# Windowed convolution with four wide tiles and one small one cut into four column phases, and the up-sampled band ahead of the next image set

## The chip, the core and the metric

The kernel runs on one core of one Trainium2 chip. The metric is the device time of one execution in microseconds, median over runs. PE is TensorE, DVE VectorE, ACT ScalarE, POOL GpSimd, SP the engine that here only issues DMAs.

## What is computed

The input x is (8, 96, 256, 256) in float32. Two layers are added to it in turn: y = x + L0(groupnorm(x)), a windowed linear attention with a batch norm, and out = y + L1(groupnorm(y)). The change touches L1 alone:

```python
for i in range(3):                      # three Haar levels
    co = haar2d(cur)                    # ll, lh, hl, hh at half the size
    cur = co[:, :, 0]
    flat = dwconv(co.reshape(B, 4 * C, h, w), wconv_w[i]) * wscale[i]      # 5x5, per channel
    level_coeffs.append(flat.reshape(B, C, 4, h, w))
next_ll = zeros
for i in reversed(range(3)):
    next_ll = ihaar2d(level_coeffs[i].at[:, :, 0].add(next_ll))
out = y + dwconv(gn_y, base_w) * base_scale + base_b + next_ll
```

## The kernel before

It has three stages. The first few tens of us build coefficient vectors (`pads`, written to `vec1` to `vec3` in DRAM by L270 to L272) and take statistics of the first image. The second, to about 5530 us, is layer 0; it writes y to `y_scratch`. The third, from about 5570 us to the end, is layer 1, and the change lies in it, but for the layout of `vec1`.

The third stage goes channel by channel, each channel in two sets of four images: 192 groups. `loop_groups` runs the same body (`steps`) on PE, ACT and DVE, each engine in its written order, joined by semaphores. An even group is the first set of a channel, an odd group the second. Level 1 and the base convolution are merged: on the full-size image they act as a 5x5 operation over pairs of rows and columns. The 256 rows are cut in five windows (`WINDOWS`), each with 52 output rows in a tile of 64 rows with halo. The two column phases (even, odd columns) lie in partitions 0 to 63 and 64 to 127, so that one tile is 128 partitions by 4 images x 128 columns = 512 elements. Each convolution of a tile (`conv(t)`) is 5 column taps x 3 matmuls (`split`, L1292 to L1294: high x high, high x low, low x high parts of a float32) = 15 matmuls of 512 columns.

One group on each engine, in order:

- PE: conv(0), conv(1); level 3 (L1325 to L1334, 20 matmuls); level 2 (30 matmuls of 256 columns); conv(2) to conv(4); a wait for `next_lo` (L1340); the up-sampling of the low band into the five windows (L1344, L1346, six matmuls of 512 columns); a wait for all five `z_lo` (L1297) and `sum_down` of the next group (L1300, ten matmuls of 512 columns into `ps_ll`).
- ACT: copy of `ps_ll` (L1263), the high parts of the level inputs (L1265, L1267), `norm` of the next group (L1243: 16 instructions from `x1` into `z`), `leading` of the next group (L1256, L1258: high parts), copy of level 3 (L1273), the high parts of the up-sampled band (L1277, L1278).
- DVE: `finish` of window 0 of the group before (L1438, two instructions a window, into `ob`), `make_in` (L1392, L1395), `finish` of window 1, `split_in` (L1402), `finish` of windows 2 to 4, `make_x1` for two groups ahead (L1369: x + gain * y), `trailing` of the next group (L1382, L1385: low parts), `up_levels` (L1409 to L1419), `split_next` (L1424, L1426; it sets `next_lo`).
- POOL, once a channel: `build` of the first level's weights when their raw DMAs have landed, and of the weights of levels 2 and 3 when level 2 of the odd group has been computed (`l2_ready`): L1185 and L1193.
- SP, in one queue: for each group, wait for `make_x1` two ahead, ten loads (`load`, L1130) for three ahead, the gain, then the five stores of this group (`store`, L1141), each behind its `finish`, which runs in the next group's turn. After an odd group's stores: the parameters, a wait for the weights of levels 2 and 3, and ten raw DMAs (`load_raw`, L1111, L1116, L1120). So the raw DMAs are issued in the turn of an even group, and that group's loads stand behind them in the queue; they are the data of the `make_x1` in the following odd group.

`xb`, `yb`, `ob` and `z` are single buffers; `zb` is double by set; `x1` has four slots.

Of the kernel before, what the change touches and what calls it, by code (L numbers as in the profile page):

```python
# [21 lines left out]
F32 = mybir.dt.float32  # L22
F32R = mybir.dt.float32r
ALU = mybir.AluOpType
# [19 lines left out]
TAPS = 5  # L44
HALF = W // 2
WROWS = 64
# [9 lines left out]
NV1 = 4 * TAPS * 2  # L56
# [7 lines left out]
CHUNKS = PIECE // 512  # L64

# [8 lines left out]
def wt_attention_kernel(nc, x, wqkv_t, wp_t, gamma, beta, base_w, base_b, base_scale, wconv, wscale,  # L74
# [10 lines left out]
    with ExitStack() as ctx:  # L85
# [128 lines left out]
        with ExitStack() as ph:  # L214
# [62 lines left out]
            def _(pool):  # L277
# [30 lines left out]
                p1 = pad1.rearrange("p (ia q dj o n) -> p ia q dj o n", ia=2, q=2, dj=TAPS, o=2)  # L308
                for ia in range(2):
                    for q in range(2):  # L310
                        for oa in range(2):
                            for p in range(2):
                                o = 1 - p
                                first = WROWS - 3 - oa
                                full = p1[:, ia, q, :, o, first:first + 2 * TAPS - 1:2]
# [5 lines left out]
                                for n, dj in enumerate(djs):  # L321
                                    lo = first + 2 * dis[0]
                                    part = p1[:, ia, q, dj, o, lo:lo + 2 * len(dis) - 1:2]
# [672 lines left out]
        with ExitStack() as ph:  # L996
# [14 lines left out]
            x1 = [sb_(f"x1_{s}", [128, PAIRW, IMGS, W]) for s in range(SLOTS)]  # L1011
# [3 lines left out]
            zb = [[sbr_(f"zb{g}_{h}", [128, WINDOWS, IMGS, ZW]) for h in range(2)] for g in range(SETS)]  # L1015
            raw1 = sb_("raw1", [128, 2 * TAPS, WROWS])
            raw2 = sb_("raw2", [128, 2 * TAPS, HALF])
            raw3 = sb_("raw3", [128, 2 * TAPS, HALF])
            mat1 = [[sbr_(f"mat1_{k}_{h}", [128, TAPS, 2 * WROWS]) for h in range(2)] for k in range(2)]
            mat2 = [sbr_(f"mat2_{h}", [128, 2, TAPS, HALF]) for h in range(2)]  # L1020
# [3 lines left out]
            down_sb = sbr_("down_sb", [128, WINDOWS, HALF])  # L1024
            UPPER = -(-(HALF // 2) // (OROWS // 2))
            LOWER = WINDOWS - HALF // OROWS
            up_sb = sbr_("up_sb", [128, UPPER + LOWER, 2 * WROWS])
            inside_sb = sb_("inside_sb", [128, PAIRW])
            mask = sb_("mask", [128, 2])
            zero1 = sb_("zero1", [128, 1])  # L1030
            z = sb_("z", [128, WINDOWS, IMGS, HALF])
# [21 lines left out]
            const_in, zeroed = sem_("constc_in"), sem_("zeroed")  # L1053
            xy_in, down_set, mask_set = sem_("xy_in"), sem_("down_set"), sem_("mask_set")
# [14 lines left out]
            NRAW = (4 + 2 + 4) * 16  # L1069
            GROUPS_C = C * SETS  # L1070

            def zero_pads(eng):
# [10 lines left out]
            def slot(k, g):  # L1083
                return 2 * k + g
# [452 lines left out]
```

## Time and profile before

| | us |
|---|---|
| median of 3 runs (lowest, highest) | 11057.21 (11053.29, 11059.47) |
| the profiled execution, its own time | 11061.64 |
| its span | 11059.8 |
| PE busy in the span | 10538.7 |
| DVE busy | 9242.7 |
| ACT busy | 7168.6 |
| POOL busy | 3679.7 |

The busy times are of the whole span, and the stages differ, so the third stage is read by itself, in a timeline of two groups. An instruction's duration counts its latency: matmuls overlap, and the pitch from one start to the next is what one costs. Times in the timelines are from the start of the span.

### The profile page before, as it was taken

Reading aid. Unit: us, or ns where it says so; the run is one execution under the profiler, and the core shown is the slowest. Engines: PE = TensorE matmul, PEld = TensorE weight load, DVE = VectorE, ACT = ScalarE, POOL = GpSimd, SP = SyncE. Lnnn points to the kernel's source line nnn. Section 1 sums busy time; section 2 is a strip of 40 time slices with the busy share of each in tenths; the row PEclk is TensorE's granted clock in tenths of the full one; section 3 lists DMA queues with packets and bytes.
Section 4 is the critical chain, followed back from the end, with each engine's and each line's share of the span. In section 5 each row is a group of like instructions: output and inputs, shape, how many; then the busy total and the mean of one; then the engine's idle time right before and its main releaser. Section 6 shows DMA issues by size and latency. Waiting matters only on the chain. (4 is left out here: it accounts for less than half of the span.)

```text
span 11059.8 us, 205333 instructions
## 1 busy us (share of the span) xinstructions
PE 10538.7 (95%) x66084; PEld 8946.0 (81%) x66084; DVE 9242.7 (84%) x16479; ACT 7168.6 (65%) x11852; POOL 3679.7 (33%) x3715
## 2 busy tenths in 40 slices
PE   4999999999999999999969999999999999999999
PEld 4888888888888888888858888888888888888887
DVE  6989989899998999988867777777777777777777
ACT  4777777777777777778735555555555555555554
POOL 3444444444444444444322222222222222222222
PEclk9999999999999999999979999999999999999999
DMA  5323333232333333322257777677777767767775
GB/s 185 133 92 126 109 109 126 92 130 95 126 114 104 114 103 115 126 81 74 69 124 154 155 156 154 154 152 155 156 157 157 155 153 156 155 153 154 152 156 125
DMA packets 1162861, 1453.43 MB, mean 131 GB/s; under 512 B 215391, under 2 KB 1125023, under 8 KB 1125279
## 3 DMA queue, kind: packets, MB, share of 16 engines
q1 hardware_dynamic: 1161055, 1442.80, 51.6%
q10 hardware_dynamic: 1376, 6.13, 0.1%
q8 instruction: 119, 1.95, 0.1%
q14 instruction: 311, 2.55, 0.1%
HBM read 1040.11 MB, written 408.56 MB: 131 GB/s over the span
## 5 line engine op out<-in xcount | busy, mean ns | idle before, releaser
L1292 PE MATMUL ps_w<-zb,mat 128*128 128x512 f32 x4800 | 1925.6, 401 | 8.6
L1293 PE MATMUL ps_w<-zb,mat 128*128 128x512 f32 x4800 | 1906.4, 397 | 0.0
L1294 PE MATMUL ps_w<-zb,mat 128*128 128x512 f32 x4800 | 1904.9, 397 | 0.0
L634 POOL CAST xn_hi<-xs 96x512 fp32r<-96x512 f32 x1024 | 840.7, 821 | 3112.3 <-PE ps_qkv L659 2261.1
L1438 DVE SCALAR_TENSOR_TENSOR ob<-ps_w,prm,x 64x512 f32<-64x512 f32 x1920 | 1440.5, 750 | 515.6 <-PE ps_w L1344 476.8
L1243 ACT ACTIVATE z<-x,prm 64x384 f32<-64x384 f32 (+1 forms) x3072 | 1814.0, 662 | 58.8 <-DVE x L1369 51.1
L1185 POOL CAST mat<-raw 128x1280 fp32r<-128x1280 f32 (+1 forms) x288 | 464.7, 1631 | 3947.6 <-DMA raw<-vec 2351.3
L657 PE MATMUL ps_qkv<-wqkv_hi,xn_hi 96*128 96x288 f32 x4096 | 1388.9, 339 | 38.2 <-POOL xn_lo L636 19.9
L636 POOL TENSOR_TENSOR xn_lo<-xs,xn_hi 96x512 fp32r<-96x512 f32 x1024 | 1363.4, 1331 | 81.8
L658 PE MATMUL ps_qkv<-wqkv_lo,xn_hi 96*128 96x288 f32 x4096 | 1214.1, 296 | 0.0
L659 PE MATMUL ps_qkv<-wqkv_hi,xn_lo 96*128 96x288 f32 x4096 | 1211.8, 296 | 0.0
L584 ACT ACTIVATE tok<-ps_qkv 128x1152 f32<-128x1152 f32 x1024 | 1160.6, 1133 | 0.0
L1292 PEld LDWEIGHTS ps_w<-zb,mat 128*128 128x128 f32 x4800 | 903.0, 188 | 302.9 <-DVE ob L1438 91.0
L552 ACT ACTIVATE att<-ps_t 96x512 f32<-96x512 f32 x1024 | 608.1, 594 | 805.2 <-PE ps_t L702 805.2
L687 PE MATMUL ps_g<-tok 128*104 128x97 f32 x8192 | 947.2, 259 | 160.2 <-DVE tok L795 160.1
L1294 PEld LDWEIGHTS ps_w<-zb,mat 128*128 128x128 f32 x4800 | 901.7, 188 | 227.0
L1293 PEld LDWEIGHTS ps_w<-zb,mat 128*128 128x128 f32 x4800 | 901.6, 188 | 209.3
L679 PE MATMUL ps_num<-kv_sb,q_sb 104*128 104x104 f32 x8192 | 1062.8, 273 | 0.0
L695 PE MATMUL ps_f<-att,wp_sb 96*96 96x512 f32 x2048 | 1052.6, 594 | 6.9 <-DVE f_cur_b L176 3.1
L679 PEld LDWEIGHTS ps_num<-kv_sb,q_sb 104*128 104x128 f32 x8192 | 1018.1, 192 | 0.0
L687 PEld LDWEIGHTS ps_g<-tok 128*104 128x104 f32 x8192 | 833.6, 172 | 222.4 <-DVE tok L795 219.7
L1263 ACT ACTIVATE ll<-ps_ll 128x512 f32<-128x512 f32 x192 | 114.8, 598 | 1373.4 <-PE ps_ll L1300 1373.4
(196 smaller groups left out, 24154.1 us busy)
## 6 DMA issues: line engine op xcount, KB each, us to landing
xst<-in_x SPq DMA_DIRECT2D x96, 2048.0 KB, 13.8
xs<-in_x SPq DMA_DIRECT2D x128, 1536.0 KB, 8.9
y_scratch<-ys SPq DMA_DIRECT2D x128, 1536.0 KB, 9.5
out<-ob SPq DMA_DIRECT2D x768, 208.0 KB
xb<-in_x SPq DMA_DIRECT2D x576, 256.0 KB
yb<-y_scratch SPq DMA_DIRECT2D x576, 256.0 KB
raw<-vec SPq DMA_DIRECT2D x192, 320.0 KB, 4.2
raw<-vec SPq DMA_DIRECT2D x384, 160.0 KB, 3.9
```

The costliest lines, as they stand in the source:

```text
L584: s_.activation(tok[:, slot].rearrange("p g (t c) -> p g t c", t=3)[:, :, :, 0:C], ps_qkv[:, :, 0:3 * C].rearrange("p g (t c) -> p g t c", ...
L636: nc.gpsimd.tensor_tensor(lo, pixels(xs, k, j), hi.bitcast(F32), ALU.subtract).then_inc(xlo_ready, 1)
L657: mm(o, hi, wqkv_hi[:], start=True, stop=False)
L658: mm(o, hi, wqkv_lo[:], start=False, stop=False)
L659: last = mm(o, lo, wqkv_hi[:], start=False, stop=True)
L679: last = mm(ps_num[:, g, 0:QR], q_sb[:, slot, g * 128:(g + 1) * 128], kv_sb[:, g // 2, :], start=True, stop=True)
L687: last = mm(ps_g[0:QR, w * GW:(w + 1) * GW], tok[:, slot, g, PART:PART + QR], tok[:, slot, g, 2 * PART:2 * PART + GW], start=g % 2 == 0, s ...
L1243: last = nc.scalar.activation(z[q * WROWS:(q + 1) * WROWS, ts, b, :], x1[slot(k, g)][rows, pairs, b, q::2], ACT.Identity, scale=prm[k][row ...
L1292: mm(out_, w[HI], xx[HI], start=start, stop=False)
L1293: mm(out_, w[HI], xx[LO], start=False, stop=False)
L1294: return mm(out_, w[LO], xx[HI], start=False, stop=stop)
L1438: last = v.scalar_tensor_tensor(out=ob[p:p + WROWS, t // 2].rearrange("p b w -> p (b w)")[:, q::2], in0=ps_w[t][q * WROWS:(q + 1) * WROWS, ...
```

## The change

The windows become four tiles of 64 rows and a fifth (`SPECIAL`) of 32 rows with 24 output rows. The fifth is cut in four column phases of 32 rows each, so it is 128 partitions by 4 images x 64 columns = 256 elements, and its convolution has three column taps (9 matmuls of 256 columns instead of 15 of 512). Its weights `mat_s` come from eight more raw DMAs a channel (`raw_s`, 16 partitions x 12 x 32 elements, runs of 128 B) and are built on POOL with the first level's; `vec1` gets two more column positions for it. Its normalised rows are written once as rows (`zn`, 4 ACT instructions of 32x256) and copied into the four phases (`zq`, 4 ACT copies of 32x256). Its share of the low band is not taken from the phases: POOL adds neighbouring columns of `zn` (`sum_columns`, 32x512), splits the sum into high and low, and PE sums these 32 rows with two matmuls of 512 columns. `finish` of the fifth is four instructions of 32x256.

Order: DVE finishes windows 0 and 1 ahead of `make_in`, and does `up_levels` and `split_next` ahead of `trailing`. ACT copies level 3 in the middle of `norm`, and splits the up-sampled band ahead of `leading`. `sum_down` waits tile by tile. No tile hangs over the image's edge any more, so the masks go, every `leading` is a plain copy and every `trailing` a subtraction. The constants for down- and up-sampling are computed on DVE and no longer loaded; only the pads of the buffers are cleared, and SP no longer waits for that before its first DMA of the stage.

```diff
-NV1 = 4 * TAPS * 2
+NV1 = 4 * (TAPS + 2) * 2
+SROWS = WROWS // 2
+SPHASES = 128 // SROWS
+STAPS = 3
+BLOCKS = W // SPHASES
+SPECIAL = WINDOWS - 1
+TILES = ((0, 0, WROWS - HALO), (WROWS + SROWS - 4 * HALO, HALO, WROWS - 2 * HALO),
+         (H - 2 * WROWS + 2 * HALO, HALO, WROWS - 2 * HALO), (H - WROWS, HALO, WROWS - HALO),
+         (WROWS - 2 * HALO, HALO, SROWS - 2 * HALO))
...
-                for t_ in (xb, yb, *zb[0], *zb[1], *in2_p, in3_hl):
-                    eng.memset(t_[:].bitcast(F32), 0.0).then_inc(zeroed, 1)
-                eng.memset(zero1[:], 0.0).then_inc(zeroed, 1)
+                for t_, n, width in padded_tiles:
+                    for at in (slice(0, n), slice(width - n, width)):
+                        eng.memset(t_[:].bitcast(F32)[..., at], 0.0).then_inc(zeroed, 1)
...
+                    for ia in range(2):
+                        for q in range(SPHASES):
+                            first = q * SROWS + ia
+                            sp.dma_start(raw_s[first:first + SROWS - 1:2, :, :],
+                                         bass.AP(tensor=vec1.tensor,
+                                                 offset=c * (NV1 * V1) + (((2 * ia + q % 2) * (2 * TAPS + 4) + q // 2 * 2) * V1
+                                                                          + (2 + WROWS - SROWS)),
+                                                 ap=[[2, SROWS // 2], [V1, SPHASES * STAPS], [1, SROWS]])).then_inc(raw_in, 16)
...
-                sp.wait_ge(zeroed, N_ZERO)
                 load_raw(0)
...
+                def sum_columns(qn, done, count, first=False):
+                    pool.wait_ge(done, count)
+                    pool.wait_ge(zn_set, qn + 1)
+                    if not first:
+                        pool.wait_ge(ll_ready, qn)
...
+                    nc.gpsimd.tensor_tensor(ls, rows_and_sums[SROWS:2 * SROWS, 0::2], rows_and_sums[SROWS:2 * SROWS, 1::2], ALU.add).then_inc(ls_set, 1)
...
+                    nc.gpsimd.tensor_copy(ls_hl[HI][:], ls).then_inc(ls_hi, 1)
...
+                    nc.gpsimd.tensor_tensor(ls_hl[LO][:], ls, ls_hl[HI][:].bitcast(F32),
+                                            ALU.subtract).then_inc(ls_lo, 1)
...
+                def channel(c, k):
+                    sum_columns(c * 2 + 1, mat23_ready, c + 1)
+                    build_first(c + 1, 1 - k)
+                    sum_columns(c * 2 + 2, mat1_ready, c + 2)
+                    build_levels(c + 1)
...
+                    for b in range(IMGS):
+                        img = IMGS * g + b
+                        last = nc.scalar.activation(
+                            zn[:, b], x1_s[own(k, g), b], ACT.Identity,
...
+                    last.then_inc(zn_set, 1)
                     for p in range(2):
-                        ts = slice(p, WINDOWS, 2)
-                        pairs = slice(0, len(range(p, WINDOWS, 2)))
+                        if p == 1 and between is not None:
+                            between()
+                        ts = slice(p, SPECIAL, 2)
+                        pairs = slice(0, SPECIAL // 2)
...
+                    for q in range(SPHASES):
+                        last = nc.scalar.activation(zq[q * SROWS:(q + 1) * SROWS].rearrange("p b j -> p (b j)"),
+                                                    rows_and_sums[SROWS:2 * SROWS, q::SPHASES], ACT.Copy)
...
-                    if n is None or n + 1 < GROUPS_C:
-                        m1, k1, g1 = ahead(m, k, g, 1)
-                        norm(m1, k1, g1)
-                        leading(qn + 1, g1)
-                    act.wait_ge(l3_ready, qn + 1)
...
+                    if more:
+                        norm(m1, k1, g1, between=copy_s3)
+                    else:
+                        copy_s3()
                     act.wait_ge(next_ready, qn + 1)
...
+                    if more:
+                        leading(qn + 1, g1)
...
                 def sum_down(qn, g):
-                    pe.wait_ge(z_lo, qn * WINDOWS + WINDOWS)
-                    for t in range(WINDOWS):
+                    for t in range(SPECIAL):
+                        pe.wait_ge(z_lo, qn * WINDOWS + (t + 1))
...
+                    pe.wait_ge(ls_lo, qn + 1)
+                    for h in (HI, LO):
+                        last = mm(ps_ll[:], down_sb[0:SROWS, SPECIAL, :], ls_hl[h][:], start=False, stop=h == LO)
                     last.then_inc(ll_ready, 1)
...
+                        if t == SPECIAL:
+                            for d in range(STAPS):
+                                split(ps_w[t][:, 0:IMGS * BLOCKS], [mat_s[k][h][:, d, :] for h in range(2)],
+                                      [zs[g][h][:, :, d:d + BLOCKS] for h in range(2)], d == 0, False)
+                            return
...
-                        finish(qn - 1, mb, kb, gb_, (0,))
+                        finish(qn - 1, mb, kb, gb_, (0, 1))
                     make_in(qn)
                     if before:
-                        finish(qn - 1, mb, kb, gb_, (1,))
+                        finish(qn - 1, mb, kb, gb_, (2,))
                     split_in(qn)
                     if before:
-                        finish(qn - 1, mb, kb, gb_, range(2, WINDOWS))
+                        finish(qn - 1, mb, kb, gb_, (3, 4))
                     if n is None or n + 2 < GROUPS_C:
                         make_x1(*ahead(m, k, g, 2))
+                    up_levels(qn)
+                    split_next(qn)
                     if n is None or n + 1 < GROUPS_C:
                         trailing(qn + 1, ahead(m, k, g, 1)[2])
-                    up_levels(qn)
-                    split_next(qn)
```

## Rows read from the trace of the kernel before

**Rows 1.** The page, part 1: busy time, share and instructions of each engine.

```profile
PE 10538.7 (95%) x66084; PEld 8946.0 (81%) x66084; DVE 9242.7 (84%) x16479; ACT 7168.6 (65%) x11852; POOL 3679.7 (33%) x3715
```

**Rows 2.** Busy time by stretches: engines' busy us (instructions), PEclk, DMA share, GB/s.

```profile
8000.00:11000.00 3000.00, 2963.87 (x14997) 2449.22 (x14996) 2344.48 (x3408) 1670.30 (x2868) 795.47 (x857) 1.00 0.71 154
```

**Rows 3.** Timeline of PE over an even group: start, us, then the instruction.

```profile
8006.38 0.97 PE L1344 MATMUL ps_w<-next_a,up_sb 128*128 128x512 f32 x3 [1.30 <-DVE next_b L1426]
...
8010.27 0.39 PE L1292 MATMUL ps_w<-zb,mat 128*128 128x512 f32 x1
...
8017.65 0.28 PE L1332 MATMUL ps<-in_hl,mat 128*128 128x256 f32 x1
...
8020.02 0.28 PE L1292 MATMUL ps<-in,mat 128*128 128x256 f32 x1
...
8023.66 0.40 PE L1292 MATMUL ps_w<-zb,mat 128*128 128x512 f32 x1
...
8034.23 0.86 PE L1344 MATMUL ps_w<-next_a,up_sb 128*128 128x512 f32 x3
...
8035.63 2.53 PE L1300 MATMUL ps_ll<-zb,down_sb 128*128 128x512 f32 x10
8038.00 0.39 PE L1292 MATMUL ps_w<-zb,mat 128*128 128x512 f32 x1
```

**Rows 4.** Timeline of DVE, the same group and the odd one behind it.

```profile
8015.03 4.61 DVE L1438 SCALAR_TENSOR_TENSOR ob<-ps_w,prm,x 64x512 f32<-64x512 f32 x6
8019.56 3.66 DVE L1369 SCALAR_TENSOR_TENSOR x<-yb,gain,xb 128x1024 f32<-128x1024 f32 x3
...
8023.81 1.88 DVE L1385 TENSOR_TENSOR zb<-z,zb 128x512 fp32r<-128x512 f32 x3
...
8026.28 0.41 DVE L1409 TENSOR_TENSOR sum<-s 128x256 f32<-128x256 f32 x1
...
8027.33 0.42 DVE L1415 TENSOR_TENSOR low<-up,ps 128x256 f32<-128x256 f32 x1
...
8055.01 1.47 DVE L1409 TENSOR_TENSOR sum<-s 128x256 f32<-128x256 f32 x1
...
8058.12 0.42 DVE L1415 TENSOR_TENSOR low<-up,ps 128x256 f32<-128x256 f32 x1
...
8060.02 1.20 DVE L1424 TENSOR_TENSOR next_a<-next_ll,next_a 64x512 fp32r<-64x512 f32 x1 [0.70 <-ACT next_a L1277]
```

**Rows 5.** Groups of ACT's instructions by form, 6000 to 9000 us: busy us, mean ns.

```profile
L1243 ACT ACTIVATE z<-x,prm 64x256 f32<-64x256 f32 x848 | 452.4, 605 | 2.8
...
L1267 ACT ACTIVATE in_hl<-in 128x256 fp32r<-128x256 f32 x107 | 44.1, 412 | 0.0
```

**Rows 6.** Timeline of POOL, the odd group: weights of levels 2 and 3.

```profile
8051.73 4.48 POOL L1185 CAST mat<-raw 128x1280 fp32r<-128x1280 f32 x2 [17.42 <-PE ps L1294]
8056.39 7.95 POOL L1193 TENSOR_TENSOR mat<-raw,mat 128x256 fp32r<-128x256 f32 x10 [0.18 <-POOL mat L1185]
```

**Rows 7.** Timeline of SP's queue in the even group: start and us of the issue.

```profile
8008.69 11.52 SPq L1141 DMA_DIRECT2D out<-ob  x5
...
8020.89 3.20 SPq L1111 DMA_DIRECT2D raw<-vec  x4
...
8029.24 0.36 SPq L1130 DMA_DIRECT2D xb<-in_x  x1
...
8030.26 0.66 SPq L1130 DMA_DIRECT2D xb<-in_x  x1
```

**Rows 8.** Busy time by stretches, as rows 2, where that group's loads end.

```profile
8042.00:8044.00 2.00, 2.00 (x10) 1.56 (x10) 1.95 (x4) 1.99 (x4) 0.00 (x0) 1.00 0.91 201
8044.00:8046.00 2.00, 2.00 (x13) 1.73 (x12) 1.92 (x4) 1.99 (x4) 0.00 (x0) 1.00 0.52 168
```

**Rows 9.** Timelines at the start of the third stage: POOL's clearing, SP's first raw DMA.

```profile
5569.57 2.66 POOL L1075 MEMSET xb<- 128x3072 f32 x1 [69.52 <-POOLq L885]
...
5586.53 2.73 SPq L1111 DMA_DIRECT2D raw<-vec  x4
```

More of the change, by code:

```diff
@@ new lines, in build_first @@
+                def build_first(c, k, first=False):
+                    pool.wait_ge(raw_in, c * NRAW + NRAW)
+                    if not first:
+                        pool.wait_ge(out_ready, c * (2 * WINDOWS) + (LEAD - 2 * WINDOWS))
+                    pool.sem_inc(pool_turn, 1)
+                    build([(mat1[k], raw1[:].rearrange("p (d o) m -> p d (o m)", o=2)[:, :, ::-1], "p d m -> p d m"),
+                           (mat_s[k], raw_s[:].rearrange("p (d o) m -> p d (o m)", o=SPHASES)[:, :, ::-1],
+                            "p d m -> p d m")],
+                          mat1_hi, mat1_ready, c + 1)
@@ L1211, in loop_groups @@
+                sum_columns(0, zeroed, N_ZERO, True)
+                build_first(0, 0, True)
+                build_levels(0)
+                with pool.Fori(0, C // 2 - 1) as m:
+                    for k in range(2):
+                        channel(m * 2 + k, k)
+                channel(C - 2, 0)
+                sum_columns(C * 2 - 1, mat23_ready, C)
             def loop_groups(eng, steps):
@@ L1436, in finish @@
                                 dve.wait_ge(prm_in[k], mc * 16 + 16)
-                        for q in range(2):
+                        for q in range(SPHASES if t == SPECIAL else 0):
+                            last = v.scalar_tensor_tensor(
+                                out=ob[0:SROWS, t // 2].rearrange("p b w -> p (b w)")[:, q::SPHASES],
+                                in0=ps_w[t][q * SROWS:(q + 1) * SROWS, 0:IMGS * BLOCKS], scalar=prm[k][own(k, g), 1:2],
+                                in1=x1_s[own(k, g)].rearrange("p b w -> p (b w)")[:, q::SPHASES],
+                                op0=ALU.add, op1=ALU.add)
+                        for q in range(0 if t == SPECIAL else 2):
                             last = v.scalar_tensor_tensor(
@@ L1471, in _ @@
[L1471 to L1476 removed]
+                v.memset(down_sb[:].bitcast(F32), 0.0).then_inc(down_set, 1)
+                v.memset(up_sb[:].bitcast(F32), 0.0).then_inc(down_set, 1)
@@ new lines, in _ @@
+                for rows, at in ((0, UPPER_AT), (64, LOWER_AT)):
+                    for t in at:
+                        start, skip, n = TILES[t]
+                        width = tile_place(t)[2]
+                        src = ident_sb[rows:rows + 64, (start + skip) // 2:(start + skip + n) // 2]
+                        for q in range(128 // width):
+                            which = at[t] + (q // 2 if t == SPECIAL else 0)
+                            for to in (0, 64):
+                                o = up_sb[to:to + 64, which, q * width + skip:q * width + skip + n]
+                                v.tensor_scalar(o.rearrange("p (a r) -> p a r", r=2), src.unsqueeze(2).to_broadcast(
+                                    [64, n // 2, 2]), 0.5, None, ALU.mult).then_inc(down_set, 1)
```

186 lines of the change are left out of this document (100 added, 86 removed).

## The prediction, written before the changed kernel was run

> **What bounds the kernel now.** I read the page first, for the engines' shares [rows 1], then the third stage alone, where the change lies: in 3000 us of it PE is busy for 2964 us, DVE for 2344, at the full clock, and the DMA engines are busy for 0.71 [rows 2]. The stretch holds 14997 matmuls and a group has 141 (75 of the convolution, 20 of level 3, 30 of level 2, 6 up, 10 down), so a group takes 28.2 us and a pair of groups (one channel) 56.4 us. Then the timeline of PE over one even group: from its first convolution at 8010.27 to the next group's at 8038.00 are 27.7 us without a wait to speak of [rows 3]. The odd groups make up the rest; ahead of 8006.38 PE stood 1.3 us for the up-sampled band, `next_lo` [rows 3]. The reason is on POOL, which builds the weights of levels 2 and 3 in the odd group, 4.5 + 7.95 us from 8051.73 on [rows 6]: in that time DVE's way from `sum` to `low2` takes 3.1 us instead of 1.05, and a subtraction of 512 elements 1.20 instead of about 0.65 [rows 4]. So PE sets the time, and the other engines' chains are late by a little, in odd groups alone.
>
> **PE.** The pitch of a 512-column matmul is (8034.23 - 8023.66) / 45 = 0.235 us, that of a 256-column one (8023.66 - 8020.02) / 30 = 0.121 us [rows 3]. The fifth window's 15 matmuls of 512 columns become 9 of 256: 3.52 - 1.09 = 2.43 us less. Up-sampling goes from 6 x 0.235 to 5 x 0.235 + 2 x 0.121, no change. `sum_down` keeps ten matmuls of 512 columns; I cost 32 instead of 128 rows at nothing. Conv(0) and conv(1) took 8017.65 - 8010.27 = 7.38 us for 30 x 0.235 = 7.05; the 0.33 is conv(1)'s wait for window 1's `finish`, which now comes ahead of `make_in` and fills DVE's wait for the down-sum. PE's work in a group is then 27.73 - 2.43 - 0.33 = 24.97 us, a pair 49.9. That is the floor, 6.5 us under 56.4. The question is who now comes late. I count from T, the end of `sum_down`. PE reaches level 3 at T + 7.05, ends it at 9.4 and level 2 at 13.05, wants `next_lo` at 21.2 and the first `z_lo` at 22.6.
>
> **ACT, even group.** Copies and level inputs end at T + 2.6. `zn` is four Identity instructions at 0.605 us or less [rows 5], overlapping by some 0.07: 2.15 us. The first half of `norm` is eight of them, 4.3 us, to T + 9.0; level 3's copy waits for PE's T + 9.4, to 10.1; the second half ends at 14.4, four `zq` copies of at most 0.41 [rows 5] at 15.9. Only then come the two splits of the band, to T + 17.2, and `leading`, one tile every 0.55. ACT's sum is some 18 us of 25, so the new instructions are hidden; were they twice as dear, the splits would end near T + 20, still ahead of PE.
>
> **DVE, even group.** The `finish` of windows 2 to 4 ended at 8015.03 + 4.61, T + 9.4 [rows 4]. One window of 1.5 us moves into the earlier wait; the fifth costs four instructions of 256 elements, bounded by half and all of 0.77 each, 1.5 to 3.1 us. I take 1.7 because the 256-element addition from PSUM is 0.42 [rows 4]. `finish` ends near T + 8.0, `make_x1` (3.66) near 11.7, `up_levels` waits for level 2 at 13.05 and gives the band at 14.4. ACT's splits then set `next_lo` at T + 18. `trailing` is 0.65 a tile (1.88 for three, overlapped [rows 4]), so `z_lo` of tile 3 comes at 20.6. PE wants them at 21.2 and 24: no stall. Even group: 25.0 us.
>
> **POOL.** `sum_columns` is two additions or subtractions of 512 elements and a cast. Its bounds are one and two times a 256-element operation (0.80 [rows 6]) each, and 0.9 for the cast (2.24 for 1280): 2.5 to 4.1 us a group, from T + 4.7 to 8.8 at the latest. PE wants it at T + 24. It contends with `split_in` for about a us, and level 3 has 2 us of room. The weights of the first level and of the fifth tile are ready long before the next channel.
>
> **SP, and the odd group.** This is what I expect to come late. The even group's stores end at 8008.69 + 11.52 = T + 9.9; the raw DMAs start at T + 10.6, the loads at 8029.24, 8.35 us later [rows 7]. Now `finish` and the last store come 1.3 us earlier, but eight raw DMAs more stand in front of the loads. No row has their form; an issue costs 0.36 to 0.80 us [rows 7]. They move 192 runs each, nearer to the load of 60 rows (240 runs, 0.36) than to `raw1` (320 runs, 0.80), with a gap: I take 0.5, so 4.0 us (2.9 to 6.4). The loads start at T + 9.3 + 8.35 + 4.0 = 21.65. Before, they had landed when the DMA share fell from 0.91 to 0.52, near 8044.7 [rows 8], 15.5 us after the first issue, two stores of this turn among them (about 2 us); with 288 rows for 304 and the stores behind them I take 13 us (12.2 to 15). That is T + 34.65, or 9.7 us after the odd group's own T', where `make_x1` could start at 8.0: DVE waits 1.7 us (0 to 6). `make_x1` ends at T' + 13.4. Now POOL is building (its start is level 2's end plus 0.4, T' + 13.4, for 12.6 us). From `sum` to the splits are 8060.02 - 8055.01 = 5.0 us, and 2.4 for the two: `next_lo` at T' + 20.8, just in time. But `trailing` now stands behind it, within POOL's build, at 1.2 us a tile: 22.0, 23.2, 24.4, 25.6 for PE's wishes 22.6 to 24.0. `sum_down` ends 0.94 after the last: T' + 26.6. Odd group 26.6, a stall of 1.6. A pair takes 51.6 us, 4.8 less; times 96: 461 us.
>
> Before, in the same place, `trailing` lay ahead of the band and was hidden under the convolution; the new order trades a late `next_lo` for a late `z_lo`.
>
> The Trainium skill, "SBUF — State Buffer", section "Who interferes with whom", says that a DVE instruction with two SBUF inputs and a GpSimd one exclude each other for the whole instruction. The slowed `sum` beside the unslowed `low2`, which reads PSUM, agrees [rows 4]; the price taken is the row's.
>
> **Start of the stage.** SP's first raw DMA waited for POOL's clearing, 5569.57 to 5586.53 [rows 9]. That wait goes, 17 us; the eight raw DMAs cost 4 back, and DVE's small constants lie under the loads. The chain from the loads to the first matmul is otherwise the same: 12 us saved (0 to 17). The longer `vec1` at the very start lies beside the statistics' loads: 0 to 3 us, taken as 0.
>
> **Sum.** 11061.6 (the profiled execution) - 461 - 12 = 10588. It stands 4.4 us above the median; so 10585.
>
> **The rivals.** (a) The raw DMAs are cheap or the loads land sooner, DVE doesn't wait, and even `trailing` is in time: the floor, 96 x 6.5 = 624 us off, 10425. For it: the DMA engines are busy for only 0.71 [rows 2]. Against: even with no wait of `make_x1`, `trailing` runs in POOL's build. (b) The queue is slower: 0.80 an issue and 15 us to land. The wait is 6 us, `next_lo` comes at T' + 25 and the odd group takes 29.3: a pair 54.3, 202 us off, 10845; with half of that, 10720. (c) DVE and POOL alternate whole instructions in `trailing`: 0.65 + 0.80 a tile instead of 1.2 is 1.0 us more a pair, 10680. (d) Slower than before: the same wait, past the point where it eats all. A us of it costs 96 us once `next_lo` is late; the pair is at 56.4 when the wait is 8.3 us, the loads landing at T' + 16.3. It takes 1.3 us an issue, or 128-byte runs that hold the DMA engines as long as 1 KB ones. At a wait of 10 us the pair is 58.1: 11210. Against: no issue in the rows costs 1.3.
>
> The Trainium skill, "DMA: Bandwidth & Descriptors", section "Specifications", gives 512 B as the least transfer at line rate, with a read-modify-write below. It speaks for (b) and (d); `raw_s` has the shortest runs of the kernel, and no row of before has 128 B.
>
> **How the numbers follow.** Forecast 0.45 (its own range 10500 to 10690), (a) 0.2, (b) 0.2, (c) 0.09, (d) 0.06. The range reaches from the floor to the middle of (b) and somewhat beyond: 10430 to 10800. 0.2%, some 22 us, is about what a measurement can tell from no change; the cases give faster 0.93, same 0.01, slower 0.06.
>
> **What would show it.** Right: even groups of 25.0 us without a wait; in odd ones DVE waits 1 to 3 us for the DMAs ahead of L1369's successor, `next_lo` isn't waited for, and PE waits in front of `sum_down` for `zb`'s low parts, 1 to 2 us. The raw issues on SP sum to about 12 us. Wrong: PE waits in even groups too, or for POOL's column sum, the issue of `raw_s` above 0.8, or a pitch of the small convolution's matmuls above 0.121.

## The result and the profile after

The changed kernel takes 11172.8 us (median of four runs, 11163.8 to 11186.5), the kernel before 11055.3 us on the same chip. The ratio is 1.011, its 95% interval 1.0095 to 1.0125. The change makes the kernel 1.1% slower, where 10585 us, some 4% faster, was forecast. The profiled execution took 11171.4 us, with a span of 11169.6.

The page of the kernel after, part 1 (busy time, share and instructions of each engine), and the first line of part 4 (the chain of work that ended last, by engine):

```profile
PE 10330.1 (92%) x65124; PEld 8796.7 (79%) x65124; DVE 9545.6 (85%) x16891; ACT 7837.5 (70%) x13388; POOL 4581.3 (41%) x4591
...
SPq 16%; DVE 15%; DMA 7%; PE 6%; issue 6%; ACT 1%; DVEq 0%; ACTq 0%
```

PE has 209 us less to do than in [rows 1], in spite of a longer run. So the work was saved, and it no longer sets the time. Before, the same line of part 4 was:

```profile
PE 28%; DVE 16%; issue 4%; ACT 1%; DMA 0%; SPq 0%; POOL 0%; DVEq 0%; POOLq 0%
```

Each chain covers about half of the span. PE had 28% of the span on it and SP's queue nothing; now SP's queue and DVE have 31%, and PE 6%.

Busy time of each engine in the same stretch of 3000 us, with the columns of [rows 2]:

```profile
8000.00:11000.00 3000.00, 2782.83 (x14095) 2313.29 (x14094) 2448.92 (x3529) 1989.37 (x3629) 1264.68 (x1298) 0.94 0.70 150
```

PE is busy for 2783 us instead of 2964, and the granted clock, 1.00 before, is 0.94. The waits between 6000 and 9000 us (engine, line and releaser: us in total, times, longest) say where it stands:

```profile
ACT ll L1336 <- PE ps_ll L1383: 534.1, 104, 6.3
...
PE ps_w L1434 <- DVE next_b L1513: 216.6, 52, 5.0
DVE x L1459 <- DMA yb<-y_scratch: 200.1, 52, 4.9
```

The first line has one wait a group: 104 groups in 3000 us, so a pair of groups takes 57.7 us (56.4 before, 51.6 forecast). The two below come 52 times, once a pair: DVE waits 3.85 us for the loads of `make_x1` (L1459), and PE 4.17 us for the band, `next_lo` (L1434). The timeline of PE shows a pair, an even group first and the odd one behind it (start, us of the instruction, idle time ahead of it):

```profile
7987.80 0.50 PE L1371 MATMUL ps_w<-zb,mat 128*128 128x512 f32 x1
...
8009.13 0.62 PE L1434 MATMUL ps_w<-next_a,up_sb 128*128 128x512 f32 x2
...
8010.73 2.08 PE L1379 MATMUL ps_ll<-zb,down_sb 128*128 128x512 f32 x8
8012.74 0.72 PE L1383 MATMUL ps_ll<-ls,down_sb 32*128 32x512 f32 x2
8013.39 0.50 PE L1371 MATMUL ps_w<-zb,mat 128*128 128x512 f32 x1
...
8034.60 0.28 PE L1373 MATMUL ps_w<-zs,mat_s 128*128 128x256 f32 x1
8039.84 1.22 PE L1434 MATMUL ps_w<-next_a,up_sb 128*128 128x512 f32 x2 [4.96 <-DVE next_b L1513]
...
8042.61 3.08 PE L1379 MATMUL ps_ll<-zb,down_sb 128*128 128x512 f32 x8
...
8046.28 0.50 PE L1371 MATMUL ps_w<-zb,mat 128*128 128x512 f32 x1
```

The even group takes 8013.39 - 7987.80 = 25.6 us and has no such wait. The odd one takes 8046.28 - 8013.39 = 32.9 us: 4.96 of waiting, and then 6.44 us for the up- and down-sampling that took 8013.39 - 8009.13 = 4.26 us in the even group. The stretches of two us around it say why (columns as above; the last three numbers are granted clock, DMA share, GB/s):

```profile
8036.00:8038.00 2.00, 0.00 (x0) 0.00 (x0) 1.28 (x3) 1.17 (x2) 2.00 (x4) 1.00 1.11 212
8038.00:8040.00 2.00, 0.16 (x1) 0.16 (x1) 1.96 (x3) 1.98 (x5) 2.00 (x3) 0.53 1.15 204
8040.00:8042.00 2.00, 2.00 (x5) 1.61 (x6) 2.00 (x3) 0.61 (x2) 0.38 (x1) 0.50 1.13 208
...
8044.00:8046.00 2.00, 2.00 (x8) 1.30 (x6) 1.95 (x3) 0.00 (x0) 0.00 (x0) 0.77 1.13 207
8046.00:8048.00 2.00, 2.00 (x9) 1.42 (x8) 0.99 (x4) 0.78 (x2) 0.00 (x0) 1.00 0.82 216
```

PE has stood still since 8034.88; from 8038 on it is granted 0.50, the 1.2 GHz level, and it has the full clock back in the stretch that begins at 8046. The wait is paid once as a wait and once more, 2.2 us, as slow matmuls.

What made the band late is read from SP's queue, then DVE, then POOL. SP, as in [rows 7], from the channel's first raw DMA to the first load, and the same place a pair later:

```profile
7997.97 3.01 SPq L1137 DMA_DIRECT2D raw<-vec  x4
8001.16 5.97 SPq L1144 DMA_DIRECT2D raw_s<-vec  x8
8007.33 1.48 SPq L1150 DMA_DIRECT2D raw<-vec  x2
8008.99 2.79 SPq L1154 DMA_DIRECT2D raw<-vec  x4
8012.11 0.62 SPq L1164 DMA_DIRECT2D xb<-in_x  x1
...
8056.34 3.01 SPq L1137 DMA_DIRECT2D raw<-vec  x4
```

DVE, the odd group, then `make_x1` of the next even group, where POOL is idle:

```profile
8027.15 4.28 DVE L1459 SCALAR_TENSOR_TENSOR x<-yb,gain,xb 128x1024 f32<-128x1024 f32 x2 [4.42 <-DMA yb<-y_scratch]
8031.46 1.64 DVE L1459 SCALAR_TENSOR_TENSOR x_s<-yb,gain,xb 32x1024 f32<-32x1024 f32 x1
8033.13 0.84 DVE L1496 TENSOR_TENSOR sum<-s 128x256 f32<-128x256 f32 x1
...
8038.66 1.13 DVE L1513 TENSOR_TENSOR next_b<-next_ll,next_b 64x512 fp32r<-64x512 f32 x1
8039.82 2.92 DVE L1472 TENSOR_TENSOR zb<-z,zb 128x512 fp32r<-128x512 f32 x4
...
8052.38 2.74 DVE L1525 SCALAR_TENSOR_TENSOR ob<-ps_w,prm,x_s 32x256 f32<-32x256 f32 x4
8055.15 2.48 DVE L1459 SCALAR_TENSOR_TENSOR x<-yb,gain,xb 128x1024 f32<-128x1024 f32 x2
8057.66 1.28 DVE L1459 SCALAR_TENSOR_TENSOR x_s<-yb,gain,xb 32x1024 f32<-32x1024 f32 x1
```

POOL, the weights of levels 2 and 3, as in [rows 6]:

```profile
8026.90 3.45 POOL L1219 CAST mat<-raw 128x1280 fp32r<-128x1280 f32 x2 [1.45 <-PE ps L1373]
8030.54 9.84 POOL L1227 TENSOR_TENSOR mat<-raw,mat 128x256 fp32r<-128x256 f32 x10 [0.18 <-POOL mat L1219]
```

A line of several instructions (`x8`) runs from the first start to the last end, gaps included. The eight new DMAs take 5.97 us of SP's queue so, and 6.2 to the start of the next DMA. The loads then start 24.3 us after the even group's T = 7987.80 and let DVE go at 8027.15, 15.0 us later. That is the moment when POOL begins its build, and `make_x1`, beside the casts and the first subtractions, takes 5.95 us instead of the 3.79 of 8055.15 to 8058.94. The band's second split ends at 8039.79, 26.4 us after T' = 8013.39, and PE was through with its convolution at 21.5.

**It closes to a circle.** From raw DMA to raw DMA: 14.1 us to the first load, 15.0 to `make_x1`, 6.0 for it, 6.7 to the end of the splits, 15.3 for `trailing`, the next group's inputs and `finish` up to 8055.12, and 1.2 for the last store and the parameters to 8056.34. From 7997.97 to 8056.34 that is 58.4 us, this pair's length (8046.28 - 7987.80 = 58.5 on PE), and PE's saved matmuls aren't on it. The steps between the splits and the end of `finish` lean on PE only through the down-sampled copy, for which DVE waits about 1 us. One more step of the circle has grown with the change: `finish` of the fifth tile, four instructions in 2.74 us, where a window in two took 1.5 ([rows 4]: 4.61 for three). No run takes that away by itself.

### The profile page after: what moved, and what is told of

The parts are those of the page before. It is cut to its first block, busy times and chain, and to the rows that moved or that the text cites. A ratio compares the mean times of both kernels' runs of the same rounds, so it can differ in the third digit from the quotient of the medians.

```text
span 11169.6 us, 210512 instructions
## 1 busy us (share of the span) xinstructions
PE 10330.1 (92%) x65124; PEld 8796.7 (79%) x65124; DVE 9545.6 (85%) x16891; ACT 7837.5 (70%) x13388; POOL 4581.3 (41%) x4591
## 4 chain that ended last, share of the span: by engine, by line
SPq 16%; DVE 15%; DMA 7%; PE 6%; issue 6%; ACT 1%; DVEq 0%; ACTq 0%
DMA yb<-y_scratch 7%; SPq L1164 5%; SPq L1144 4%; DVE x L1459 3%; PE ps_ll L1379 2%; SPq L1137 2%; DVE ob L1525 2%; SPq L1154 2%; DVE ob L1531 2%; DVE x_s L1459 2%; SPq L1150 1%; PE ps_w L1436 1%; PE ps_w L1434 1%; DVE next_b L1513 1%; DVE sum L1496 1%
## 5 line engine op out<-in xcount | busy, mean ns | idle before, releaser
L1317 ACT ACTIVATE z<-x,prm 64x256 f32<-64x256 f32 x3072 | 1640.6, 605 | 15.1
L1371 PE MATMUL ps_w<-zb,mat 128*128 128x512 f32 x3840 | 1546.6, 403 | 1.2 <-DVE ob L1531 1.2
L1373 PE MATMUL ps_w<-zb,mat 128*128 128x512 f32 x3840 | 1526.6, 398 | 0.0
L1372 PE MATMUL ps_w<-zb,mat 128*128 128x512 f32 x3840 | 1524.8, 397 | 0.0
L1531 DVE SCALAR_TENSOR_TENSOR ob<-ps_w,prm,x 64x512 f32<-64x512 f32 x1536 | 1151.5, 750 | 34.9 <-PE ps_w L1434 5.1
L1227 POOL TENSOR_TENSOR mat<-raw,mat 128x256 fp32r<-128x256 f32 (+1 forms) x1248 | 1155.6, 959 | 34.7 <-POOL mat_s L1219 17.4
L801 DVE TENSOR_REDUCE ss<-sq 128x64 f32<-128x768 f32 x1024 | 965.8, 943 | 18.2 <-ACT sq L594 17.7
L717 PEld LDWEIGHTS ps_t<-ident_sb,att_t 128*96 128x96 f32 x4096 | 480.7, 125 | 612.4 <-issue 611.7
L1459 DVE SCALAR_TENSOR_TENSOR x<-yb,gain,xb 128x1024 f32<-128x1024 f32 x384 | 585.4, 1565 | 407.6 <-DMA yb<-y_scratch 404.6
## 6 DMA issues: line engine op xcount, KB each, us to landing
xst<-in_x SPq DMA_DIRECT2D x96, 2048.0 KB, 13.8
```

The source lines that it names most:

```text
L1317: last = nc.scalar.activation(z[q * WROWS:(q + 1) * WROWS, ts, b, :], x1[slot(k, g)][rows, pairs, b, q::2], ACT.Identity, scale=prm[k][row ...
L1371: mm(out_, w[HI], xx[HI], start=start, stop=False)
L1372: mm(out_, w[HI], xx[LO], start=False, stop=False)
L1373: return mm(out_, w[LO], xx[HI], start=False, stop=stop)
L1531: last = v.scalar_tensor_tensor(out=ob[p:p + WROWS, t // 2].rearrange("p b w -> p (b w)")[:, q::2], in0=ps_w[t][q * WROWS:(q + 1) * WROWS, ...
```

## The experiments

Two theories stood at first. By the **queue theory** the eight DMAs ahead of the loads make `make_x1` late, and this sets the time. By the **port theory** DVE and POOL hold each other up, and the order in which the loads come matters little. Ratios are to the kernel before on the same chip, with their 95% intervals. The edits are to the kernel after unless said otherwise.

**The raw DMAs moved behind the loads.** In SP's program, inside the even group, and taken out at the end of the channel:

```diff
                         if g == 0 and more:
                             load_gain(m * 2 + (k + 2), k)
+                    if g == 0 and raw:
+                        sp.wait_ge(mat23_ready, m * 2 + (k + 1))
+                        load_raw(m * 2 + (k + 1))
                     store(m * 2 + k, g, m * 4 + (2 * k + g))
...
                         load_prm(m * 2 + (k + 2), k)
-                        sp.wait_ge(mat23_ready, m * 2 + (k + 2))
-                        load_raw(m * 2 + (k + 2))
```

> The changed kernel, with the eighteen raw DMAs of an even group issued behind that group's ten loads instead of ahead of them. Queue theory (the odd group is late because its data stand behind the raw DMAs): the loads start some 8 us earlier, DVE's wait for them in front of make_x1 (200 us in 3000 us) goes, the odd group falls from 32.9 to 25 to 28 us, the whole to 10,450 to 10,800 us. Port theory (the odd group is late because DVE and POOL want SBUF together while POOL builds): the wait for the loads goes, but the odd group keeps 30 us or more and the whole stays above 10,950. The weights come later here, so a wait of level 3 for them would be a cost of this edit of its own.

It took 11027.4 us, ratio 0.9992 (0.9982 to 1.0001): 1.2% off the kernel after, and no more. DVE no longer waits for loads, and PE no longer for the band. But the weights now arrive late, and their build slides into the odd group's `trailing`. DVE, then POOL, in that place, and one wait of PE:

```profile
8039.87 6.13 DVE L1471 TENSOR_TENSOR zb<-z,zb 128x512 fp32r<-128x512 f32 x4
...
8049.88 1.48 DVE L1478 TENSOR_TENSOR in<-ll 128x256 f32<-128x256 f32 x2
```

```profile
8040.95 3.37 POOL L1218 CAST mat<-raw 128x1280 fp32r<-128x1280 f32 x2
8044.50 8.20 POOL L1226 TENSOR_TENSOR mat<-raw,mat 128x256 fp32r<-128x256 f32 x10 [0.18 <-POOL mat L1218]
```

```profile
PE ps_ll L1378 <- DVE zb L1471: 73.1, 116, 0.9
```

Four tiles of `trailing` take 6.13 us, 1.5 each, where they took 2.92 in the kernel after; `in<-ll` takes 1.48 instead of 0.77. Moving the queue's load turned a late transfer into a longer overlap of DVE and POOL. The queue is a cause, but undoing it in this way pays back the gain; each theory was half right.

**The eight DMAs left out** (only channels 0 and 1 fetch them; the others use the fifth tile's weights of channel 1):

```diff
+                    if not small:
+                        sp.sem_inc(raw_in, 8 * 16)
-                    for ia in range(2):
+                    for ia in range(2 if small else 0):
                         for q in range(SPHASES):
```

> The changed kernel, with the eight raw_s DMAs issued for channels 0 and 1 only; later channels use the fifth tile's weights of channel 1, so the output is not the reference's. It takes away 6.0 us of issue and the 128-byte runs, and leaves the order as it is. Queue theory: the loads start 6 us earlier, DVE's wait falls from 3.9 us in an odd group to nothing, and the whole to 10,550 to 10,750 us. Port theory: the whole falls by less than 250 us.

10714.7 us, ratio 0.9711 (0.9694 to 0.9727). By the two ratios that is 0.0399 x 11055 = 441 us less than the kernel after. The waits for the loads and for the band are gone from the head of the list, and the clock in the stretch is 1.00. The eight DMAs alone, issue and transfer together, cost 441 / 96 = 4.6 us a pair.

**The wait replaced by work.** If PE's wait is only a symptom of the circle, 20 more matmuls in its place cost nothing; and if the half clock behind it matters, they even win:

```diff
+                    if g == 1:
+                        pe.wait_ge(ll_copied, qn + 1)
+                        for _i in range(20):
+                            mm(ps_ll[:], down_sb[:, 0, :], zb[g][HI][:, 0, :, 2:2 + HALF], start=True, stop=True)
                     pe.wait_ge(next_lo, qn + 1)
```

> The changed kernel, with 20 matmuls of 512 columns into the free ps_ll put in front of PE's wait for the up-sampled band in odd groups, 4.7 us of work that nobody uses. Clock theory (after the 5 us wait PE runs at half its clock for some 6 us more, which costs 2.2 us an odd group): the wait becomes work of the same length, the granted clock stays at 1.0, and the whole falls by about 96 x 2.2 = 210 us, to 10,960. If the slower matmuls had another cause, or the clock no part in it, the time stays at 11,170 or rises.

11097.2 us, ratio 1.0054 (1.0037 to 1.007). The timeline of PE at that place, and DVE's wait from 6000 to 9000 us:

```profile
8011.03 4.88 PE L1430 MATMUL ps_ll<-zb,down_sb 128*128 128x512 f32 x20
8016.18 0.73 PE L1438 MATMUL ps_w<-next_a,up_sb 128*128 128x512 f32 x2 [0.28 <-DVE next_b L1517]
...
8017.88 2.08 PE L1379 MATMUL ps_ll<-zb,down_sb 128*128 128x512 f32 x8
```

```profile
DVE x L1463 <- DMA yb<-y_scratch: 256.5, 53, 5.4
```

PE now stands still for 0.28 us, `sum_down` runs at full speed (2.08 instead of 3.08), and yet only 75 us are won (62 by the ratios), 0.8 a pair at most, not the 2.2 that the half clock costs PE. DVE simply waits longer for the loads, 4.8 us instead of 3.85. This is the plainest evidence for the circle: PE can be given 4.9 us more work in every pair, and the kernel gets faster. The little that is won fits DVE's wait for the down-summed copy, which from 6000 to 9000 us fell from 86.8 to 58.2 us. My expectation took the clock's 2.2 us for time on the path; only the 1 us for which DVE waits on PE's down-sum was.

**The eight DMAs added to the kernel before**, in the same place of SP's queue, into memory that has no use in this stage:

```diff
                     for ia in range(2):
+                        for q in range(4):
+                            first = q * 32 + ia
+                            sp.dma_start(extra[first:first + 31:2, :, :],
+                                         bass.AP(tensor=vec1.tensor,
+                                                 offset=c * (NV1 * V1) + (((2 * ia + q % 2) * 8 + q // 2 * 2) * V1 + 34),
+                                                 ap=[[2, 16], [V1, 12], [1, 32]])).then_inc(raw_in, 16)
+                    for ia in range(2):
```

> The kernel before, with eight more raw DMAs of the form of raw_s (16 partitions, 12 runs of 128 B) a channel, in the place in the queue where the changed kernel has them, into a space that nobody reads any more. Queue theory: the loads of the even group start 6 us later, the next odd group's make_x1 waits 3 to 5 us for them and slides into POOL's build, and PE waits in odd groups: the whole rises by 150 to 700 us over the kernel before, which has a longer group (28.2 us) and so some 3 us more room. If the queue is harmless, the time stays within 50 us of the kernel before.

11445.5 us, ratio 1.0356 (1.0339 to 1.0374). SP's queue, then DVE:

```profile
8021.37 5.97 SPq L1120 DMA_DIRECT2D outer<-vec  x8
...
8032.12 0.37 SPq L1139 DMA_DIRECT2D xb<-in_x  x1
```

```profile
8047.26 3.67 DVE L1378 SCALAR_TENSOR_TENSOR x<-yb,gain,xb 128x1024 f32<-128x1024 f32 x3 [1.49 <-DMA yb<-y_scratch]
```

The same 5.97 us, the same 15 us to land (8032.12 to 8047.26), and a wait of `make_x1` that the kernel before doesn't have in its odd group:

```profile
8047.29 3.66 DVE L1369 SCALAR_TENSOR_TENSOR x<-yb,gain,xb 128x1024 f32<-128x1024 f32 x3
```

The eight cost 401 us, 4.2 a pair, without any other part of the change. `make_x1` itself is not slowed in this place (3.67 us against 3.66), so this is the queue's part almost by itself.

**Most of the contention taken away.** Levels 2 and 3 built with two subtractions instead of ten from the second channel on, so that the other low parts stay those of the first channel:

```diff
-                        for d in range(0, raw.shape[1], 2):
+                        for d in range(0, 2 if light else raw.shape[1], 2):
```

> The changed kernel, with POOL's build of the weights of levels 2 and 3 cut from ten subtractions to two from the second channel on (the other low parts stay those of channel 0, so the output is not the reference's). The queue is as it is. Queue theory alone: the loads land as late as before, make_x1 starts as late, the time falls by less than 200 us. Port theory alone: without POOL beside them make_x1, the way from sum to low2 and the splits of the odd group take their undisturbed times, 5 to 6 us less, PE's wait goes and with it the half clock, and the whole falls by 500 us or more, to 10,650. I expect both: what lies beside the eight subtractions left out is some 4 us of DVE, so 10,700 to 10,850.

10947.3 us, ratio 0.9909 (0.9893 to 0.9926): 225 us, less than I had expected. The waits between 6000 and 9000 us:

```profile
DVE x L1459 <- DMA yb<-y_scratch: 218.2, 54, 5.2
...
PE ps_w L1434 <- DVE next_b L1513: 148.7, 55, 3.1
```

DVE waits for the loads as in the kernel after. The two casts, which lie right over `make_x1`, were left in (its instructions of 128x1024 average 1.58 us in both kernels), and so was the queue.

**The new order undone**: `trailing` ahead of the band again, and on ACT `norm` and `leading` ahead of level 3's copy and the splits.

```diff
-                    up_levels(qn)
-                    split_next(qn)
                     if n is None or n + 1 < GROUPS_C:
                         trailing(qn + 1, ahead(m, k, g, 1)[2])
+                    up_levels(qn)
+                    split_next(qn)
```

> The changed kernel with the old order: DVE does trailing ahead of up_levels and split_next, ACT does all of norm and leading ahead of level 3's copy and the band's splits. The tiles, the raw DMAs and the column sum stay. In the odd group make_x1 ends late either way; with trailing (3 to 5 us) in front, the band comes later by that, and PE's wait for it grows from 5 to 8 to 10 us: the whole rises by 200 to 450 us, to 11,400 to 11,600. If the new order were what costs, the time would fall towards 10,900 instead.

11740.6 us, ratio 1.0625 (1.0608 to 1.0643). The wait for the band, from 6000 to 9000 us:

```profile
PE ps_w L1432 <- DVE next_b L1511: 450.8, 95, 8.2
```

It now comes in every group, even ones too. The new order isn't the cause; without it the change costs 568 us more.

**The eight DMAs on ACT's queue**, four at the end of each group, after `leading`. The function is SP's own loop, with the engine as an argument:

```diff
                     if more:
                         leading(qn + 1, g1)
+                    if g == 0 and (n is None or 0 < n < GROUPS_C - 2):
+                        load_raw_s(act, m * 2 + (k + 1), (1,))
+                    if g == 1 and (n is None or n < GROUPS_C - 4):
+                        act.wait_ge(mat1_ready, m * 2 + (k + 2))
+                        load_raw_s(act, m * 2 + (k + 2), (0,))
```

> The changed kernel with the eight raw_s DMAs issued by ACT, four at the end of each group, so that SP's queue holds what it held before the change; every byte still moves and the output is the reference's. Queue theory, by issue: the loads start 6 us earlier, as when the eight are left out (10,715), DVE's wait for them goes; ACT, with 7 us of room in a group, pays 3: 10,700 to 10,820, a kernel faster than both by 2 to 3%. If it is the transfer of the 128-byte runs that made the loads late, and not their issue, the wait stays and the time is above 11,000.

10896.9 us, ratio 0.9858 (0.9841 to 0.9874), 1.4% under the kernel before with all its output. Timeline of DVE in the odd group, then one of the new issues on ACT:

```profile
8032.22 2.91 DVE L1468 SCALAR_TENSOR_TENSOR x<-yb,gain,xb 128x1024 f32<-128x1024 f32 x2
...
8043.68 4.55 DVE L1481 TENSOR_TENSOR zb<-z,zb 128x512 fp32r<-128x512 f32 x4
```

```profile
8015.81 0.63 ACTq L1123 DMA_DIRECT2D raw_s<-vec  x1
```

`make_x1` starts without a wait, and `trailing`, which now lies in POOL's build, takes 4.55 us instead of 2.92. The same bytes in the same short runs are moved; only their place in a queue differs. The Trainium skill, "DMA: Bandwidth & Descriptors", section "Specifications", gives 512 B as the least transfer at line rate. In this run the 128 B runs kept no load from DVE, so what had delayed the loads was mostly the issue time ahead of them; in the kernel after, too, each of the eight had landed 2.1 to 2.3 us after its issue. What is left over the kernel without these DMAs is 182 us (162 by the ratios). It shows on PE in part as waits for the tiles' low parts, 37.2 us from 6000 to 9000 us, and for the band, 23.2 us, where the kernel without the eight has 1.2 and none: a smaller form of the stall for `z_lo` that was forecast, now that the loads are in time. Whether ACT's issues, the transfers, or the later build of the first level's weights bring it about, no run tells.

**Both causes removed**: the last kernel with the light build.

> raw_s on ACT's queue as in the run before (10,897) and POOL's build of levels 2 and 3 with two subtractions instead of ten (low parts of channel 0 stay, so the output is not the reference's). If late loads and POOL beside DVE are the whole cause, almost nothing is left over PE's own work: a pair of groups 50 to 51 us, granted clock 1.0, 10,430 to 10,550 us. If a third cause is hidden (ACT's longer chain, the fifth tile's finish, the down-sum in pieces), the time stays above 10,600 and its wait shows in the trace.

10572.4 us, ratio 0.9577 (0.956 to 0.9594). The same wait as above counts the groups:

```profile
ACT ll L1340 <- PE ps_ll L1392: 460.9, 117, 4.6
```

117 groups in 3000 us, 25.6 each: the even group's length of the kernel after, now for all. No wait of PE is among the ten longest, and the clock of the stretch is 1.00. So the queue and the overlap of DVE with the eight subtractions are together what stood between the change and PE's own pace. The two casts are still there, and beside them DVE is still slowed, but within its slack.

**A version that keeps all the work.** Level 3's weights built as soon as level 3 is done, level 2's after level 2, with the eight DMAs on ACT:

```diff
+                    if not first:
+                        pool.wait_ge(l3_ready, c * 2)
+                        pool.sem_inc(pool_turn, 1)
+                    build([(mat3, raw3[:, :, ::-1], "p s d m -> p (s d) m")], mat23_hi, None, c * 2 + 1)
                     pool.wait_ge(l2_ready, c * 2 + 1)
                     pool.sem_inc(pool_turn, 1)
-                    build([(mat2, raw2[:, :, ::-1], "p s d m -> p (s d) m"),
-                           (mat3, raw3[:, :, ::-1], "p s d m -> p (s d) m")],
-                          mat23_hi, mat23_ready, c + 1)
+                    build([(mat2, raw2[:, :, ::-1], "p s d m -> p (s d) m")], mat23_hi, mat23_ready, c * 2 + 2)
```

> raw_s on ACT's queue, and the build of levels 2 and 3 in two: level 3's weights as soon as level 3 of the odd group is done (3.6 us earlier), level 2's then. The same POOL work, ended near T' + 22 instead of T' + 26. If what counts is that trailing lies in the build, trailing gets free and the time falls by 50 to 150 us under 10,897, to 10,750 to 10,850. If the chain through make_x1 and the band counts as much, that is delayed by 1 to 2 us in return, and the time is the same within 50 us or higher.

10825.3 us, ratio 0.9803 (0.9786 to 0.9821). It beats the kernel before by 2.0% and, by the two ratios, 0.9803 / 1.011, the kernel after by 3.0%. Against the kernel with the eight DMAs on ACT alone it wins 72 us.

**The new order alone, on the kernel before**: one more window of `finish` ahead of the inputs, the band ahead of `trailing`, `copy_s3` inside `norm`, `leading` last. The heart of the edit:

```diff
-                    if n is None or n + 1 < GROUPS_C:
-                        trailing(qn + 1, ahead(m, k, g, 1)[2])
                     up_levels(qn)
                     split_next(qn)
+                    if n is None or n + 1 < GROUPS_C:
+                        trailing(qn + 1, ahead(m, k, g, 1)[2])
```

> The kernel before with the new order alone: finish of windows 0 and 1 first, the band ahead of trailing on DVE, level 3's copy inside norm and leading last on ACT, the down-sum waiting tile by tile. Tiles, DMAs and POOL are those of before. The 0.33 us wait of conv(1) goes in every group; the band is no longer late in odd groups (about 1.0 us); trailing, five tiles in POOL's build, may be late instead. I expect 20 to 130 us less than before, 10,910 to 11,020. If the new order itself costs (ACT's chain, late trailing), the time is the same or up to 150 us more.

10921.4 us, ratio 0.9892 (0.9874 to 0.991). The order is worth 1.1% by itself, with PE's work unchanged. Two parts of the change thus pull against each other: this order wins 120 us on the kernel before, and the eight DMAs that the cheaper fifth tile needs take some 400 to 440 away.

## Why the prediction was wrong

**What held.** PE's account: 9 matmuls of 256 columns in 1.09 us, and a forecast even group of 25.0 us that measured 25.6. The missing 0.6 is spread over the convolution's pitch and the up- and down-sampling; the two matmuls of 32 rows, which I had costed as part of ten at 0.235, take 0.65 together. Even groups have no stall, ACT's work is hidden, POOL's column sum is never waited for, and the new order frees PE's way. The floor of 10425 was 0.6 x 192 = 115 us too low: 10540, with 10572 measured once both causes are away.

**The step that failed is "SP, and the odd group".** Its terms, counted from T of the even group or T' of the odd one:

| term | forecast | measured |
|---|---|---|
| first raw DMA | T + 9.3 | T + 10.2 |
| issue of the eight `raw_s` DMAs | 4.0 us | 6.2 us |
| first load issued to `make_x1` | 13 us | 15.0 us |
| `make_x1` | 3.66 us | 5.95 us |
| `make_x1` end to splits' end | 7.4 us | 6.7 us |
| `next_lo` | T' + 20.8 | T' + 26.4 |
| PE's wait for it | 0 | 4.2 us (mean) |
| up- and down-sampling after it | 3.8 us | 6.4 us |
| stall for `z_lo` | 1.6 us | none |

The first row is `finish` of the fifth tile, 2.74 us where I took 1.7. The second went by the number of runs, and by two numbers of [rows 7] that don't measure the same. The 0.36 us of a load of 60 rows is one instruction, without the gap behind it. `raw1`'s 3.20 / 4 = 0.80 is a line of four with the gaps between. The eight measured 6.17 / 8 = 0.77 from start to start, close to `raw1`, which I had as the dear end. With 0.80 and 15 us to land, rival (b) gave T' + 25 and 10845 us. Its inputs came true and its sum did not, since two terms were in no case at all.

The first is `make_x1` itself. I priced DVE against POOL for `sum`, the splits and `trailing`, and wrote that POOL's build starts when `make_x1` ends. Once the loads were late, `make_x1` came to lie beside the casts instead. Before, it lay just ahead of the build: in the odd group from 8047.29 for 3.66 us, the casts from 8051.73 on [rows 6]. The rule of the Trainium skill that the prediction cites ("SBUF — State Buffer", "Who interferes with whom": a DVE instruction with two SBUF inputs contends with a GpSimd one that reads SBUF) covers it, for its inputs are `yb` and `xb`. This case's trace agrees: 3.79 us beside an idle POOL, 5.95 beside the casts and the first subtractions.

The second is the clock. The prediction had no price for what a wait of PE does to the work behind it. Nearly 5 us idle gave 0.50 for about 6 us.

None of the four signs that were to show the forecast wrong came: PE doesn't wait in even groups or for the column sum, the issue stayed under 0.8, and the small matmuls' pitch was 0.121. Of those that were to show it right, DVE's wait came (3.85 us), but PE waits for `next_lo` and not for `zb`'s low parts.

**The sum, redone.** The pair was forecast at 51.6 us and took 57.7. Twice 0.6 of PE's pace, minus the `z_lo` stall of 1.6, plus 4.2 of waiting and 2.2 of slow matmuls make 6.0 of these 6.1; 96 x 6.1 = 586 us on 10585 is 11171, against 11172.8 measured. (The stage's first convolution starts at 5625.4 us instead of 5643.4, 18 us earlier where I took 12; with that the sum is 11165.) On PE's side this is bookkeeping, not cause: the run with the wait filled shows that the wait and the clock are mostly what the circle leaves over.

**The rival that came true** is (d), the one on the slow side, with a chance of 0.06. Its mechanism held: the loads behind the raw DMAs make `make_x1` late until all the gain is eaten. It put break-even at landing at T' + 16.3 and 1.3 us an issue. The loads landed at T' + 13.8 with 0.77 an issue, and the two missing terms, 2.3 and 2.2 us, made up for the rest. The chance was small because that threshold, worked out without the two terms, was set too high.

**Deeper** than a term lies how the sum was made. I laid each engine's work on a ruler that began at PE's T and T', and asked who is late for PE. I never asked what makes SP's turn begin: `finish` and the last store, which end 15 us after the splits that had themselves waited for the loads. When such a chain leads back to its own start, a delay isn't absorbed by the next even group's slack, and the pair is as long as the circle, whatever PE saves.

## What to carry to other kernels

Before PE's work is cut, follow one buffer's way round: transfer, consumer, what the consumer releases, the store, and the queue back to the transfer; if that circle is nearly as long as PE's pace, every DMA issue put into it costs its full time once the slack is used up, and the saved matmuls buy nothing. Put small transfers that aren't needed soon on the queue of an engine with slack, and price a queue by the measured time from one issue's start to the next, at the nearest shape on the dear side. When something comes late, check what it will newly run beside: here the late instruction met another engine's build, which cost another 2.3 us.

## What the runs showed of the hardware that was not expected

- An issue of the new form took 0.58 us by itself on SP (the kernel after) and 0.59 on ACT (median of 16 each), and 0.77 from one start to the next on either, although one moves only 192 runs of 128 B. On SP, `raw1`'s (320 runs) took 0.60 by themselves and 0.80 from start to start, the loads of 64 rows 0.60 to 0.65 and 0.74. So moving the eight to ACT made none of them cheaper; it took them out from in front of the loads.
- How much DVE and POOL take from each other depends on how their instructions meet. One addition of `sum`, 0.43 us alone, took 0.84 in the kernel after and 3.78 beside the end of a subtraction and two casts in the kernel with both causes removed (timeline of DVE there):

```profile
8032.34 3.78 DVE L1505 TENSOR_TENSOR sum<-s 128x256 f32<-128x256 f32 x1
```

- ACT's copy of 32x256 elements out of a strided place took more time than a contiguous one with four times the partitions, 661 ns against 401 (groups by form, 6000 to 9000 us; columns: busy us, mean ns, idle before). The prediction had taken at most 0.41; it lay in ACT's slack:

```profile
L1323 ACT ACTIVATE zq<-rows_and_sums 32x256 f32<-32x256 f32 x416 | 274.8, 661 | 4.9
...
L1331 ACT ACTIVATE zs<-zq 128x256 fp32r<-128x256 f32 x104 | 41.7, 401 | 0.0
```
